# A ViT tower in one TensorE queue: stage order before the gates redrawn, w1 centred in four pieces, values of half 1 on ScalarE, bias as second-layer product, the end by tile groups

## The reference, cut to what matters

```python
h = einsum('bnk,ek->bne', patches, W) + b                       # 768 -> 64
q, k, v = h @ Wq.T, h @ Wk.T, h @ Wv.T                          # 64 -> 64
s = softmax((q k^T - (1 - mask) * 1e10) * 64 ** -0.5, axis=1)   # over the queries
h = layernorm(h + s @ v)
top2 of h @ gate_w + gate_b (16 experts); weights = softmax(top2)
e = relu(h @ w1[e] + b1[e]) @ w2[e] + b2[e]                     # 64 -> 128 -> 64
y = h + sum of the two chosen e, weighted
y = (y - mean) / sqrt(var + eps) * gamma + beta
out = layernorm(h + y)
```

## Time and profile before

| | |
|---|---|
| median of 3 runs | 62.47 us (62.45 to 65.4) |
| profiled execution | 62.52 us |
| its span, first to last instruction | 60.7 us |
| mean granted TensorE clock | 0.971 |
| TensorE matmul busy | 50.5 us, 83% |
| VectorE, ScalarE busy | 23.2 us, 23.7 us |
| GpSimd busy | 5.0 us, all in the first 6 us |
| DMA | 3.31 MB, all input in the first 14 us |

### The profile page before, as it was taken

One profiled execution on the slowest core, in us unless ns is written; L12 is line 12 of the kernel. 1 busy time (PEld: TensorE's weight loads), 2 busy tenths in 40 slices (PEclk: granted clock), 3 DMA queues, 4 the chain that ended last, 5 costly groups with the idle time before them and its releaser, 6 DMA issues.

```text
span 60.7 us, 1021 instructions
## 1 busy us (share of the span) xinstructions
PE 50.5 (83%) x377; PEld 27.8 (46%) x378; DVE 23.2 (38%) x90; ACT 23.7 (39%) x64; POOL 5.0 (8%) x23
## 2 busy tenths in 40 slices
PE   2999999999989999999999954999999999770000
PEld 0425538747625467746563623354675454150000
DVE  1041203234804935133806194054352381604620
ACT  1701030563268402825555062109640907714320
POOL 6998000000000000000000000000000000000000
PEclk9999999999999999999999999999999999999855
DMA  0799998710000000000000000000000000020002
GB/s 0 209 351 349 392 312 182 194 49 11 0 0 0 0 0 0 0 0 11 0 0 0 5 0 0 5 0 0 0 0 0 0 11 0 0 49 0 0 0 49
DMA packets 1915, 3.31 MB, mean 54 GB/s; under 512 B 757, under 2 KB 949, under 8 KB 1845
## 3 DMA queue, kind: packets, MB, share of 16 engines
q1 hardware_dynamic: 1830, 3.18, 17.5%
q10 hardware_dynamic: 80, 0.07, 0.4%
HBM read 3.09 MB, written 0.15 MB: 53 GB/s over the span
## 4 chain that ended last, share of the span: by engine, by line
PE 77%; DVE 9%; ACT 8%; issue 2%
PE banks L556 13%; PE banks L564 12%; PE banks L582 9%; PE banks L537 7%; PE banks L462 6%; PE banks L576 4%; PE banks L511 3%; PE banks L480 2%; PE banks L545 2%; PE banks L468 2%; PE banks L473 2%; PE banks L571 2%; PE banks L519 2%; ACT hid L252 2%; PE banks L492 2%; PE banks L486 2%
## 5 line engine op out<-in xcount | busy, mean ns | idle before, releaser
L252 ACT ACTIVATE hid<-banks 128x576 f32<-128x576 f32 x16 | 10.0, 645 | 10.3 <-PE banks L556 10.3
L385 DVE TENSOR_TENSOR xg<-banks,y1T 128x288 f32<-128x288 f32 x16 | 6.7, 453 | 13.8 <-PE banks L537 12.2
L556 PE MATMUL banks<-xg,w1c 64*128 64x288 f32 x64 | 10.2, 431 | 0.0
L564 PE MATMUL banks<-hid,w_sb 128*64 128x288 f32 x64 | 10.0, 422 | 0.0
L556 PEld LDWEIGHTS banks<-xg,w1c 64*128 64x128 f32 x64 | 5.6, 186 | 3.6 <-DVE xg L385 2.1
L582 PE MATMUL banks<-zeros 128*128 128x512 bf16 x17 | 5.9, 498 | 1.2 <-DVE zeros L405 1.2
L564 PEld LDWEIGHTS banks<-hid,w_sb 128*64 128x64 f32 x64 | 3.7, 135 | 4.7 <-issue 1.8
L537 PE MATMUL banks<-gT,sel 64*128 64x288 f32 x28 | 4.9, 425 | 0.0
L340 DVE TENSOR_REDUCE var<-sq 72x4 f32<-72x256 f32 x6 | 2.5, 414 | 5.5 <-ACT sq L225 5.5
L582 PEld LDWEIGHTS banks<-zeros 128*128 128x128 bf16 x18 | 1.9, 118 | 4.4 <-issue 2.5
L462 PE MATMUL banks<-xk,tokwb_sb 128*64 128x288 f32 x24 | 3.9, 447 | 0.0
(11 more groups left out here) (88 smaller groups left out, 58.2 us busy)
## 6 DMA issues: line engine op xcount, KB each, us to landing
xk<-x_kt SPq DMA_DIRECT2D x6, 288.0 KB, 4.5
w1x_sb<-w1x SPq DMA_DIRECT2D x1, 524.1 KB
w_sb<-w SPq DMA_DIRECT2D x1, 512.0 KB, 8.9
tokwb_sb<-tokw SPq DMA_DIRECT2D x1, 192.5 KB, 2.6
out<-fin SPq DMA_DIRECT2D x2, 72.0 KB
small_sb<-small ACTq DMA_DIRECT2D x1, 64.5 KB, 3.0
```

The source lines that it names most:

```text
L252: nc.scalar.activation(hid[:, h, 2 * p:2 * p + 2, :], p_hid[:, slot:slot + 2, :], ACT.Relu).then_inc(hid_ready, 1)
L385: nc.vector.tensor_tensor(xg[:, h, p, :], p_gb[p % GB], y1T[:, h, :], ALU.mult).then_inc(xg_ready, 1)
L556: mm = nc.tensor.matmul(p_hid[:, 2 * (p % RING) + r, :], w1c[rows, p, :], xg[rows, h, p, :], start=True, stop=True)
L564: mm = nc.tensor.matmul(p_moe[h][D * r:D * (r + 1), :], w2_sb[:, e, :], hid[:, h, e, :], start=(p == 0), stop=(p == PAIRS - 1))
```

## The change

It redraws the order of the stages and touches these parts:

1. SyncE no longer issues the embedding weights; ScalarE does, ahead of the small weights.
2. The products of the gamma and beta constants go behind the last embedding, the mask product of half 1 behind the gate product, and VectorE's copies of the constants behind the values of half 0.
3. `w1_centre` makes four pieces of 256 columns instead of two of 512, in banks 3, 0, 1, 4, and stands behind the transposition of half 0. `keep_warm(2, 0)` and `keep_warm(8, 0)` become one `keep_warm(3, 5)`.
4. The copy of yT of half 0 goes to VectorE. The values of half 1 are scaled on ScalarE, tile by tile; VectorE still inverts the sums.
5. Residual and attention of half 1 come ahead of the first gate spreadings. Half 1's norm, transposition, logits and gates come earlier in the lists of all three engines, and `gates` is cut into `gates_top` and `gates_out`.
6. b2 is padded to 128 rows and travels as a seventeenth block of w2; the bias product goes over 128 rows.
7. From `moe_add` to the output, half 1 is worked in two groups of two tiles (`ENDS`), each with its own bank, semaphore counts and output transfer; half 0 stays one group.

```diff
-    WG = 2
-    PG = PAIRS // WG

+    PG = 2
+    WG = PAIRS // PG
...
-        p_w1 = [banks[:, b, :] for b in (2, 3)]
+        p_w1 = [banks[:, b, 0:PG * F] for b in (3, 0, 1, 4)]
...
-        p_cc = [tiles(b, 2 * D) for b in (4, 5)]
+        p_cc = [tiles(b, 2 * D) for b in (4, 5, 6)]
+        ENDS = ((0, 0, NT, p_cc[0]), (1, 0, NT // 2, p_cc[1]), (1, NT // 2, NT, p_cc[2]))
...
@@ sync @@
-            sp.dma_start(tokwb_sb[:, :], tokw).then_inc(tokw_in, 16)
...
-            for h in range(HALVES):
-                sp.wait_ge(fin_ready, h + 1)
-                sp.dma_start(out_v[h], fin[:, h, :, :]).then_inc(out_done, 16)
+            for k, (h, t0, t1, _) in enumerate(ENDS):
+                sp.wait_ge(fin_ready, k + 1)
+                sp.dma_start(out_v[h][:, t0:t1, :], fin[:, h, t0:t1, :]).then_inc(out_done, 16)
...
@@ scalar @@
+            act.dma_start(tokwb_sb[:, :], tokw).then_inc(tokw_in, 16)
             act.dma_start(small_sb[:, :], small).then_inc(small_in, 16)
...
+            def values(h):
+                act.wait_ge(srec_ready, h + 1)
+                act.wait_ge(v_psum, h + 1)
+                for t in range(NT):
+                    ins = nc.scalar.activation(vs[:, h, t, :], p_v[h][:, t, :], ACT.Copy, scale=srec[:, h, t:t + 1])
+                ins.then_inc(vs_ready, 1)
...
+            def squares2(k):
+                h, t0, t1, cc = ENDS[k]
+                act.wait_ge(cc_psum, k + 1)
+                nc.scalar.activation(sq[:, h, 1, t0:t1, :], cc[:, t0:t1, 0:D], ACT.Square,
+                                     scale=D ** -0.5).then_inc(sq_ready[1], 1)
...
-            def moe_copy(h):
+            def moe_copy(k):
+                h, t0, t1, _ = ENDS[k]
+                cols = slice(TT * t0, TT * t1)
                 act.wait_ge(moe_psum, h + 1)
-                nc.scalar.copy(moe[D:P, h, :], p_moe[h][D:P, :]).then_inc(moe_ready, 1)
+                nc.scalar.copy(moe[D:P, h, cols], p_moe[h][D:P, cols]).then_inc(moe_hi_ready, 1)
...
             moe_copy(1)
+            moe_copy(2)
             squares2(1)
-            inverse_deviation(1, 1)
-            squares3(1)
-            inverse_deviation(1, 2)
+            squares2(2)
+            inverse2(1)
+            inverse2(2)
+            squares3(1)
+            squares3(2)
+            inverse3(1)
+            inverse3(2)
...
@@ vector @@
+            def sums_inverse(h):
                 dve.wait_ge(e_ready, NT * (h + 1))
                 nc.vector.reciprocal(srec[:, h, :], ssum[:, h, :]).then_inc(srec_ready, 1)
...
+            def yT_copy(h):
+                dve.wait_ge(yT_psum, h + 1)
+                nc.vector.tensor_scalar(y1T[:, h, :], p_yT[h], 1.0, None, ALU.add).then_inc(yT_ready, 1)
...
@@ tensor @@
-                nc.tensor.matmul(p_moe[h][0:D, :], b2, gT[0:D, h, :], start=False, stop=False)
+                nc.tensor.matmul(p_moe[h][0:D, :], w2_sb[:, E, :], gT[:, h, :], start=False, stop=False)
...
-            scores(1)
-            w1_centre(0)
             pe.wait_ge(gate_ready, 1)
             y1_transpose(0)
-            keep_warm(2, 0)
-            pe.wait_ge(w1_ready, 1)
+            w1_centre(0)
             logits(0)
             w1_centre(1)
-            keep_warm(8, 0)
-            gates_spread_first(0)
-            pe.wait_ge(e_ready, 2 * NT)
-            gates_transpose(0)
-            gates_spread_first(1)
-            pe.wait_ge(w1_ready, 2)
-            experts_in(0, 0)
-            experts_in(0, 1)
+            w1_centre(2)
+            w1_centre(3)
+            keep_warm(3, 5)
             pe.wait_ge(vs_ready, 2)
             residual(1)
             attend(1)
+            gates_spread_first(0)
+            pe.wait_ge(e_ready, 2 * NT)
+            gates_spread_first(1)
+            pe.wait_ge(w1_ready, WG)
+            gates_transpose(0)
+            experts_in(0, 0)
+            experts_in(0, 1)
```

More of the change, by code:

```diff
@@ L57, in vit_tower @@
         gatex = w1x_sb[:, E * F:E * F + E]
-        w2_sb = sb("w2_sb", [F, E, D])
-        wq, wk, wv, b2 = (small_sb[:, D * k:D * (k + 1)] for k in range(4))
-        gamma, beta = (small_sb[:, 4 * D + k:4 * D + k + 1] for k in range(2))
+        w2_sb = sb("w2_sb", [F, E + 1, D])
+        wq, wk, wv = (small_sb[:, D * k:D * (k + 1)] for k in range(3))
+        gamma, beta = (small_sb[:, 3 * D + k:3 * D + k + 1] for k in range(2))
         ident = sb("ident", [TT, TT])
@@ L280, in _ @@
             squares1(0)
[L281 removed]
+            inverse1(0)
+            exps(1)
             w1_copy(0)
[L283 to L284 removed]
             gate_exp(0)
             w1_copy(1)
+            values(1)
+            w1_copy(2)
+            w1_copy(3)
+            squares1(1)
+            inverse1(1)
             gT_copy(0)
@@ L410, in _ @@
             nc.vector.tensor_copy(wv2[:, :], p_wv).then_inc(wv_ready, 1)
+            t_copy(0)
+            softmax_max(0)
+            sums_inverse(0)
+            values(0)
             dve.wait_ge(cgc_psum, 1)
@@ L413, in _ @@
             nc.vector.tensor_copy(betac[:, :], p_betac).then_inc(cgc_ready, 1)
-            t_copy(0)
-            softmax_max(0)
-            values(0)
-            variance(0, 0)
+            variance1(0)
             t_copy(1)
@@ L422, in _ @@
             softmax_max(1)
-            gates(0)
+            yT_copy(0)
+            gates_top(0)
+            sums_inverse(1)
+            gates_out(0)
             gate_tokens(0, 0)
+            variance1(1)
             gate_tokens(0, 1)
-            values(1)
+            norm1_out(1)
             gate_tokens(0, 2)
             gate_tokens(0, 3)
-            variance(1, 0)
+            gates_top(1)
             gate_tokens(0, 4)
             gate_tokens(0, 5)
-            norm1_out(1)
+            gates_out(1)
+            dve.wait_ge(cgc_ready, 2)
+            y1_beta(0)
             gate_tokens(0, 6)
             gate_tokens(0, 7)
-            dve.wait_ge(cgc_ready, 2)
-            y1_beta(0)
-            gates(1)
+            y1_beta(1)
             for p in range(4):
@@ L442, in _ @@
             gate_tokens(1, 5)
-            variance(0, 1)
+            variance(1, 0)
             gate_tokens(1, 6)
@@ L595, in _ @@
             embed(0, 0)
-            pe.wait_ge(gcen_ready, 1)
-            for r in range(2):
-                nc.tensor.matmul(p_cgc[D * r:D * (r + 1), :], cen2[0:D, :], gcen[:, :], start=True, stop=True)
-            nc.tensor.matmul(p_betac, bc(beta, [D, TT]), cen2[0:D, :], start=True, stop=True).then_inc(cgc_psum, 1)
             embed(0, 1)
@@ L611, in _ @@
             embed(1, 2)
-            mask_scores(1)
+            pe.wait_ge(gcen_ready, 1)
+            for r in range(2):
+                nc.tensor.matmul(p_cgc[D * r:D * (r + 1), :], cen2[0:D, :], gcen[:, :], start=True, stop=True)
+            nc.tensor.matmul(p_betac, bc(beta, [D, TT]), cen2[0:D, :], start=True, stop=True).then_inc(cgc_psum, 1)
             attend(0)
@@ L645, in _ @@
             experts_in(0, 3)
+            logits(1)
             gates_spread(0, 2)
```

142 lines of the change are left out of this document (82 added, 60 removed).

## The result

The changed kernel takes 57.16 us against 62.46: 0.9155 of it, 95% interval 0.9125 to 0.9184. The profiled execution took 57.21 us with a span of 55.4. Forecast were 58.2 us and 57.2 to 59.8, so the time lies just under the range. Ratios leave disturbed executions out; where a kernel's own times vary by more than some 2%, they are given one by one.

The account below looks back on a forecast made before the run. It took TensorE's one queue of products to bound the kernel. Its terms, 0.05 - 1.60 - 1.79 - 0.95 = -4.29, taken from 62.52, gave 58.2 us, range 57.2 to 59.8.

Parts of the forecast that it names:

- I take 0: Start: small weights, issued behind the embedding weights on ScalarE's queue, cost TensorE no wait; 0 us.
- Start, +0.05: Start and attention: same products in another order, scores of half 1 may wait for VectorE; +0.05 us, bounds 0 and 0.44.
- the other end of my bounds: Start: small weights landing 4.5 us after issue, like the median x part, at 5.7; TensorE would wait 0.9 us.
- From 16.13 to the gates, -1.60: From 16.13 to the first general gate spreading: 7 fillers and the y1T wait go, two small waits come; -1.60 us.
- Experts of half 0, -1.79: Experts of half 0: wait for g goes (-1.49), gated tokens late (+0.1), cheaper gate spreadings (-0.4); -1.79 us.
- The end, -0.95: End of half 1 in two groups of two tiles: last product at 57.67 against 58.62; -0.95 us, bounds -1.3 and +0.2.
- the walk: End, from the fin of half 0: step times summed by durations, from first add 53.1 to last product 57.67 us.
- New waits: Rival: values on ScalarE, gT copy and gated tokens 4 come late and hold up products; +1.1, 59.3 us; chance 0.14.
- The end without gain: Rival: the end in two groups gains 0 instead of -0.95; 59.2 us; chance 0.09.
- Small weights late: Rival, at the start: the small weights land late and TensorE waits; +0.9, 59.1 us; chance 0.05.
- The clock: Rival: with 7 fillers less around 17 to 21 us TensorE falls to 1.2 GHz; 63.8 us; chance 0.03.

Follow-up runs that it names:

- small_weights_first: Changed kernel with the small weights issued ahead of the embedding weights on ScalarE's queue; 56.2 us, 0.9018 of the kernel before.
- before_bias_128_rows: Kernel before with only b2 as a seventeenth block of w2 and the bias product over 128 rows; 61.9 us, 0.991 of the kernel before.
- no_filler_after: Changed kernel with the small weights first and 0 instead of 3 fillers; 0.9711 of the kernel before, and between 60.2 and 63.0 us.
- three_fillers_before: Kernel before with 3 instead of 10 fillers between the stages; 67.1, 67.6, 67.8 and 69.5 us, 1.0812 of the kernel before.

## Why the prediction was off

The direction, the places and the signs of the terms were right; the sum missed by 1.04 us and the range by 0.04. Two steps failed, in opposite directions. One is "I take 0" for the small weights: it cost 0.6 us more than forecast. The other is the pricing of the products in the new order by their old rows, with the bias and the last transfer put at nothing and the end sized too small: the gains came out 1.6 us larger. That the forecast missed by no more than 1.04 us is luck, since the first error hid part of the second. Term by term:

- Start, +0.05: failed, +0.66. The step was "I take 0, by the row of the same transfer" for the small weights. They landed 4.7 us after their issue, 0.2 us later than even the other end of my bounds had it, and TensorE waited 1.27 us. The row was not quite of the same transfer either: it carried 64.5 KB before and 48.5 KB now, and was still slower. The engines are shared with x in either order of the queue; what my two ends left out is that 192.5 KB stood ahead on the same queue. That this cost only half of the wait has a reason that I hadn't: the small products took 0.45 instead of 0.62 us and the six embedding products 1.61 instead of 2.05. These durations are those of TensorE's higher level (2.4 GHz); the granted clock reads 1.00 over the whole start in both kernels, over the fillers of 0.45 us too, so there the level can be read from durations only. small_weights_first shows what the error was worth: 0.95 us.
- From 16.13 to the gates, -1.60: the mechanism was right, the size -2.09. The 7 fillers went, and products stand where most of them had filled a wait. ScalarE's four values took 0.93 instead of 1.1, and TensorE waited 0.20. Mis-sized were the changes from one form of product to the next: transposition 0.26 instead of 0.40, both first gate spreadings in a row 1.15 instead of 1.30, two pairs of first layer 1.17 behind a transposition instead of 1.31 behind a gate spreading. I had carried the old prices into a new order. The old prices, here and in the next stretch:

```profile
21.82 0.65 PE banks L545 x16
...
23.52 1.31 PE banks L556 x8
...
31.29 0.40 PE banks L505 x4
...
34.12 0.55 PE banks L519 x7
...
37.30 0.47 PE banks L526 x4
```

- By the Trainium skill (ScalarE: Activation LUTs, Rules for kernel authors) these four would, by estimate, have taken 1.4 us. They took 0.93, so that budget is too high for these four in a row.
- Experts of half 0, -1.79: right in the wait for g (1.49, gone; the new wait is 0.04) and in the sum of the gate spreadings (0.46 for 0.4), though the one behind the logits still cost 0.65. What it had at nothing: the logits cost 0.40 instead of 0.55, the transposition of the gates 0.40 instead of 0.47, and "The bias as a product over 128 instead of 64 rows has the same 288 columns: nothing" was wrong by some 0.2 in this half and 0.15 in the next. before_bias_128_rows shows it alone, with 0.15 in each.
- The end, -0.95: the mechanism was right, the size -1.16, and the smaller last transfer gave 0.19 that I had at nothing. Counted from the fin of half 0, the walk was right to 0.1 up to the last squares (3.44 us; they ended at 3.40) and 0.2 too long from there to the last exponential, because neighbours overlap on ScalarE: the last logarithm starts at 52.66, 0.09 before the end of the exponential that began at 52.55.
- Rivals. New waits: none over 0.2 but that for the small weights, which had a rival of its own. The end without gain: no. Small weights late: it came true. The gains of the other terms were underrated by 1.6 us in all, and 0.6 of that went into the start. The clock: it did not occur in the changed kernel (granted clock 1.00 from 16 to 36 us), but I had it at 0.03, and the three kernels with fewer fillers show that it stood close. Its evidence against, 1.49 us of nothing at 1.00 in the earlier trace rows, was thin: in three of six profiles the same wait was followed by half clock. The price I gave it, 5.6 us, lies between the 4.0 and 6.8 us that no_filler_after took above small_weights_first.
- One reading was off, and nothing hung on it: the digits of the earlier trace rows stand at 9 from the second slice to the 34th, with one 8 and the dip, and at 7 in the 35th and 36th.

On the rule that transpositions do not count as busy in the same way as other products (the Trainium skill, TensorE: Matmul & The Clock Gate, Part 4: PE-mode transpose): no run here separates transpositions from idle time and small products, so none shows it.

Left open: when TensorE comes to 2.4 GHz in the start. Six embedding products from 5.41 us on took 1.65, 1.78, 2.06, 2.22 or 2.48 us in kernels whose start is the same, and I can't say whether the rest of the program or chance decides. So a single execution can be off by up to 0.8 us for its start alone, which is why the chains and not only the times are compared here. Nor did the runs settle what of the idle time and the small products takes the clock down when the fillers are gone.

## What to carry to other kernels

When stages are redrawn, price each product by its neighbour in the new order, not by its old row: here some 0.6 of the 1.6 us of underrated gains lay there, and another 0.3 to 0.4 in the bias products, which overlap with the second layer next to them once both use all 128 rows and different columns. A filler that seems to stand in a wait may be holding the clock for the next 10 us; before it is taken out, real products must stand there (0.4 us of idle time was enough to lose the clock in two of four executions), and the granted clock behind it, in more than one execution, is the row to look at. Whether a filler stands in a wait is read from when the value behind it is ready, not from its own duration. A small transfer that the first products wait for goes ahead of a large one on its queue.

## What the runs showed of the hardware that was not expected

- A 48.5 KB transfer behind one of 192.5 KB on the same queue landed 4.7 us after its issue; ahead of it, 3.4; alone on its queue beside others, 2.9.
- 0.9 us of idle TensorE in a stretch of small products was followed by some 14 us at 1.2 GHz (no_filler_after); with three fillers the kernel before took 67.1 to 69.5 us, longer than three of its four runs with none.
- A wait of 1.5 us of TensorE was followed by a granted clock of 0.50 in three profiles and of 1.00 in three others. The kernel before and three_fillers_before have the same order around it and fell on different sides.
- Four instructions of 72x64 in a row on ScalarE took 0.93 us, and the next logarithm began 0.09 us before the end of an exponential.
- A bias product over 128 rows into columns 0 to 63 lets the next second-layer product into the other columns start beside it (1.60 us for bias and four products); over 64 rows it did not (1.75).
